# A causal mask taken from TensorE to POOL's select, with new turns for all engines

## The chip, the cores and the metric

The kernel runs on one core of a Trainium2 chip. The metric is device time in microseconds (us) from one launch; lower is better. All times are of that core.

## The reference

A residual stream `x` of 2048 tokens and 128 features goes through four layers. Each computes `x = x + s * silu(f)`, where `s` and `f` are two branches on the layer-normalised `x`.

- Layer 0: `s` is a Mamba-2 block; `f` a mixture of 8 experts (2 per token) with 2 shared experts, all with biases.
- Layer 1: `s` is gated linear attention; `f` a feed-forward with ternary weights.
- Layer 2: gated linear attention; and again 8 experts, 2 per token, with a shared one.
- Layer 3: `s` is causal softmax attention with rotary positions, 16 heads of 8 features, over sequences of 256 tokens; `f` is a short gated recurrence and an output projection.

What the change touches is the attention of layer 3:

```
scores = einsum('bhqd,bhkd->bhqk', q, k) * hd ** -0.5
mask   = where(kpos > qpos, -inf, 0)
attn   = softmax(scores + mask, axis=-1)
out    = einsum('bhqk,bhkd->bhqd', attn, v) ; out = out @ Wo.T
```

and, in layer 0, the sum of the experts' second biases, weighted by the gates, and the shared experts' biases.

## The kernel before

**Tiling and order.** Tokens go in four blocks (`tb`) of 512 per layer, each of two sequences of 256 (`bb`). Every engine has its program as a set of named streams of Python generators; a `yield` ends a turn. The strings in `ORDER` say, engine by engine, which stream takes the next turn and how many ("Y3" is three turns of stream Y), and `follow` deals them out. So each engine's instruction order is fixed beforehand, across layers, and engines meet only by semaphores. `T`, `S`, `V`, `G` are the counters of TensorE, ScalarE, VectorE and POOL (GpSimd). A turn beyond a stream's end, and the first turn of each part of a chain, issue nothing. The streams that matter: A (input side of the attention branch), B (its output side), F (the `f` branch and experts), R and C (sending rows to the experts, fetching them back), M (`peaks3`), Y (`attn3`); on sync, H moves layer 3's heads through DRAM and M its maxima.

**Layer 3's attention.** `heads3` computes rotated queries and keys, splits them into bf16 parts and sends them through DRAM (`part`, SP lines L2391 and L2413) into the head layout `qp`, `kp`. The head buffers of block `tb` are those of `tb - 2`, so the trip of a later block waits for the last score unit of that block. `peaks3` (TensorE L744 to L769, VectorE L1966) computes the masked scores once to find each row's maximum: score products L754 and L760, mask products L756 and L761 (identity times `mts[0]`, which adds -1e30), one VectorE reduction L1971 for each unit. The maxima travel by DMA into rows 72 and 73 of `qp`, so that the second pass has them subtracted in its product.

`attn3` is the second pass. A block has 24 units: for each of two sequences `bb` and four groups `g` of four heads, `k` = 0 and 1 (two heads each, 256 queries by the first 128 keys) and `k` = 2 (four heads, second half by second half). A unit is one turn of scores into bank 3 or 6, transposed (keys on rows): L782 or L788, with the mask product L784 or L789 (`mts[1]`) on each diagonal block. ScalarE takes the exponential into one of four tiles `PT` (L1278). `values` has a turn for each unit: nothing for `k` = 0, for `k` = 1 the products L800 (four heads in four 32-column strips of the array, side by side, into bank 7), for `k` = 2 the products L805. The ninth value column is one, which yields the softmax's sum. ScalarE copies bank 7 out (L1285), TensorE turns it (L814, `norm`), VectorE divides (L1997, L2002). At a block's end `tail` transposes (L521) and multiplies by Wo (L529). `used_up` says when an exponential may overwrite its `PT` tile.

**Layer 3's recurrence** is L989, L990 on TensorE with ScalarE L1407 to L1412 and VectorE L2122 to L2127; its last part is L1418 and L1420.

**Between layers 2 and 3.** POOL fetches expert answers row by row with indirect DMAs (`fetch`, L2270, 16 for each half of the tokens); VectorE mixes them by the gates (L2081), ScalarE takes the tanh of the gate (L1298), VectorE updates `x`. From 640 us on POOL has three rsqrt steps (L2171, L2175) and nothing else.

**Layer 0's bias.** In `shared`, before the second products L854 of each of four chunks, L851 multiplies `cmT` (10 rows: eight gate weights and two ones, by token) with `bias0` (10 x 128). 16 such products in the kernel, two records each.

## Time and profile before

| what | value |
|---|---|
| time, median of 3 runs | 764.8 us (761.33, 764.8, 766.14) |
| profiled execution, first to last instruction | 796.7 us |
| TensorE busy | 691.7 us (87%) |
| VectorE busy | 500.9 us (63%) |
| ScalarE busy | 439.9 us (55%) |
| POOL busy | 252.8 us (32%) |
| mean granted TensorE clock | 0.931 of 2.4 GHz |

The profiled execution is longer than the timed ones; its span is the time against which its durations add up. PE is TensorE, ACT ScalarE, DVE VectorE, SP the sync engine. Busy time counts pipelined matmuls up to their modelled ends, so the time from one start to the next says more about their cost than their duration. A releaser after `<-` is the instruction whose end ended the idle time.

### The profile page before, as it was taken

To read this page: it belongs to the slowest core of one execution; us is meant where nothing else is said; L and a number is where in the kernel's file an instruction comes from. 1 tells how busy PE (TensorE), PEld (TensorE's weight loads), DVE (VectorE), ACT (ScalarE), POOL (GpSimd) and SP (SyncE) were. 2 spreads that over 40 slices of the span, in tenths; PEclk is the share of its full clock that TensorE was granted. 3 is DMA by queue.
4 is the path that set the end of the run, shared out by engine and by line. 5 is a ranking of instruction groups with operands and counts; after the bars stand their busy time and mean duration, and the time that the engine had idled before them with its cause. 6 is when DMAs were issued, how large, how long until landed. Compare 5 with 4: busy or idle time off the path is not lost.

```text
span 796.7 us, 13833 instructions
## 1 busy us (share of the span) xinstructions
PE 691.7 (87%) x5174; PEld 538.4 (68%) x5174; DVE 500.9 (63%) x1333; ACT 439.9 (55%) x944; POOL 252.8 (32%) x267
## 2 busy tenths in 40 slices
PE   7699898899888689899799993989877699999996
PEld 4377666578766567677679983789756466767663
DVE  1747877449965774868643863447646568767652
ACT  4535787449884665685535652134541265655554
POOL 1473456552515812323650326354000520000000
PEclk9679999999999897999989997889998889999998
DMA  9721654126301130000126662427894603306100
GB/s 305 226 63 32 180 145 140 42 87 176 91 24 44 50 124 1 1 0 2 34 89 220 209 196 70 163 77 225 262 250 135 154 15 101 62 21 143 28 17 14
DMA packets 71217, 83.94 MB, mean 105 GB/s; under 512 B 7199, under 2 KB 55914, under 8 KB 71146
## 3 DMA queue, kind: packets, MB, share of 16 engines
q1 hardware_dynamic: 67054, 74.65, 32.3%
q0 software_dynamic: 4096, 8.40, 3.5%
q8 instruction: 41, 0.67, 0.3%
q14 instruction: 26, 0.21, 0.1%
HBM read 65.46 MB, written 17.43 MB: 104 GB/s over the span
## 4 chain that ended last, share of the span: by engine, by line
PE 64%; DVE 10%; ACT 9%; DMA 6%; issue 4%; POOL 4%; another core or an unknown queue 1%; SPq 0%; ACTq 0%; POOLq 0%; DVEq 0%
PE bank L854 4%; PE bank L842 4%; PE bank L922 4%; PE bank L713 4%; PE bank L931 4%; PE bank L690 2%; PE bank L667 2%; PE bank L529 2%; DMA part<-arena 2%; PE bank L896 2%; PE bank L800 2%; PE bank L782 2%; PE bank L659 2%; PE bank L958 2%; DMA W<-part 2%
## 5 line engine op out<-in xcount | busy, mean ns | idle before, releaser
L1971 DVE TENSOR_REDUCE arena<-bank 128x2 f32<-128x512 f32 (+1 forms) x96 | 63.7, 684 | 25.7 <-PE bank L756 15.7
L1278 ACT ACTIVATE arena<-bank 128x512 f32<-128x512 f32 x96 | 55.8, 597 | 34.0 <-PE bank L784 27.3
L931 PE MATMUL bank<-room,h 128*128 128x128 f32 x368 | 50.6, 281 | 4.8 <-DVE h L2054 1.6
L922 PE MATMUL bank<-room 128*128 128x128 f32 x368 | 50.3, 282 | 2.6 <-DMA room<-in_wx 2.5
L931 PEld LDWEIGHTS bank<-room,h 128*128 128x128 f32 x368 | 46.0, 195 | 7.7 <-issue 3.3
L922 PEld LDWEIGHTS bank<-room 128*128 128x128 f32 x368 | 46.3, 197 | 5.3 <-DMA room<-in_wx 3.6
L1374 ACT ACTIVATE h<-bank,room 128x128 f32<-128x128 f32 x96 | 27.3, 368 | 27.3 <-PE bank L922 18.1
L2270 POOL DMA_INDIRECT win<-answer,arena x24 | 23.6, 984 | 57.9 <-DMA answer<-room 38.4
L2255 POOL DMA_INDIRECT sent<-own,arena x32 | 32.5, 1015 | 27.7 <-DVE arena L1647 18.8
L2171 POOL TENSOR_SCALAR rs<-mv 128x4 f32<-128x4 f32 x20 | 7.3, 363 | 105.5 <-DVE mv L1459 82.0
L2255 POOL DMA_INDIRECT sent<-own,room x32 | 36.1, 1128 | 12.0 <-issue 8.3
L1915 DVE TENSOR_TENSOR arena<-bank,cst 128x512 f32<-128x512 f32 x32 | 21.1, 686 | 28.9 <-remote 11.1
L1305 ACT ACTIVATE h<-bank,col 128x512 f32<-128x512 f32 x24 | 16.3, 686 | 40.3 <-PE bank L842 24.7
L1737 DVE SCALAR_TENSOR_TENSOR arena<-arena,col 128x512 f32<-128x512 f32 x48 | 35.4, 770 | 3.4 <-ACT arena L1094 3.4
L2270 POOL DMA_INDIRECT room<-answer,room x32 | 32.6, 1017 | 14.4 <-issue 8.1
L2054 DVE TENSOR_SCALAR h<-bank,room 128x128 f32<-128x128 f32 x88 | 24.7, 343 | 16.2 <-PE bank L922 13.2
L713 PE MATMUL bank<-xt,arena 128*128 128x64 f32 (+1 forms) x128 | 19.0, 299 | 16.3 <-DVE arena L1915 13.5
L713 PEld LDWEIGHTS bank<-xt,arena 128*128 128x128 f32 x128 | 19.2, 226 | 20.6 <-DVE arena L1915 15.5
L1337 ACT ACTIVATE h<-bank,room 128x128 f32<-128x128 f32 x92 | 26.6, 382 | 3.6 <-PE bank L886 3.4
L1247 ACT ACTIVATE arena<-bank 128x512 f32<-128x512 f32 (+1 forms) x16 | 7.8, 489 | 36.9 <-PE bank L713 36.9
L2175 POOL TENSOR_TENSOR sc<-sc,mhalf 128x16 f32<-128x16 f32 (+1 forms) x12 | 27.8, 2317 | 0.9
L896 PE MATMUL bank<-room,h 128*128 128x128 f32 x184 | 27.0, 293 | 1.0 <-ACT room L1346 1.0
(413 smaller groups left out, 2059.1 us busy)
## 6 DMA issues: line engine op xcount, KB each, us to landing
room<-in_wx SPq DMA_DIRECT2D x46, 578.0 KB
room<-in_wx SPq DMA_DIRECT2D x46, 257.0 KB, 2.8
answer<-room SPq DMA_DIRECT2D x44, 128.0 KB
room<-sent SPq DMA_DIRECT2D x20, 256.0 KB
W<-part SPq DMA_DIRECT2D x12, 384.0 KB
room<-part SPq DMA_DIRECT2D x12, 384.0 KB
sent<-acc SPq DMA_DIRECT2D x10, 256.0 KB, 4.3
part<-arena SPq DMA_DIRECT2D x12, 128.0 KB
```

What stands on the lines that cost most here:

```text
L713: mm = pe.matmul(b[:, o + dv * h:o + dv * h + dv], AT[:, h, c, :], vv[:, c, dv * h:dv * h + dv], start=(q == 0), stop=(q == 0 or h == 3))
L842: mm = pe.matmul(b[:], w1[:, q // nh, width(q % nh)], src[:], start=True, stop=True)
L854: mm = pe.matmul(o, hid(l, tb, q)[:, width(c)], w2[:, q // nh, q % nh, :], start=(q == 0 and l == 2), stop=(q == 3))
L896: mm = pe.matmul(b[:, width(i)], hid(0, "x", u)[:, width(2 * i + j)], zw2[slots(0, v)][:, j, :], start=(j == 0), stop=(j == 1))
L922: mm = pe.matmul(b[:, width(j)], xw1[slots(2, u)][:, width(j)], xsT[(s // 2) % 2][:, width(s % 2)], start=True, stop=True)
L931: mm = pe.matmul(banks[6][:, width(s % 2)], hid(2, "x", u)[:, width(j)], xw2[slots(2, u)][:, j, :], start=(j == 0), stop=(j == 3))
L1278: act.activation(PT[n % 4], banks[(3, 6)[n % 2]][:], ACT.Exp).then_inc(*S.step("PT", tb, n))
L1737: dve.scalar_tensor_tensor(out=xj, in0=raw[:, j, :, k:k + 256], scalar=K("conv_w", 4 * j + k), in1=xj, op0=ALU.mult, op1=ALU.add).then_inc ...
L1971: dve.tensor_reduce(mx[:, tb % 2, bb, int(k < 2), h:h + nh], banks[1 + n % 2][:].rearrange("p (h t) -> p h t", h=nh), AX.X, ALU.max).then_ ...
L2175: pool.tensor_tensor(dst, dst, mhalf[:, 0:src.shape[1]], ALU.pow).then_inc(*G.step(*name))
L2255: pool.indirect_dma_start(sent[h], bass.IndirectOffsetOnAxis(ap=place[l, h][:, n:n + 1], axis=0), own[:, h, n % 8, :], None).then_inc(*DMA ...
L2270: pool.indirect_dma_start(gx[l][4 * k + c], None, answer[h], bass.IndirectOffsetOnAxis(ap=place[l, h][:, n:n + 1], axis=0)).then_inc(*DMA[ ...
```

## The change

1. **The mask of `attn3`.** L784 and L789 are gone; the score products now end their accumulation. POOL has a new stream Y: behind each exponential it runs `affine_select` in place on the diagonal blocks of the `PT` tile (2 blocks of 128 columns for `k` = 0 and 1, 4 for `k` = 2), which writes zero where the key is later than the query. `peaks3` keeps its mask products; one mask tile `mts` is left.
2. **Value products.** `values(i)` is one turn per group: all eight products, behind the select of the group's third unit. It stands behind the scores of unit 3i + 5 (before: behind those of 3i + 3 and 3i + 4). `norm(i)` stands behind the scores of unit 3i + 8. `PT` has six tiles (`N_P`), `used_up` counts groups, and ScalarE's copy of bank 7 stands behind the exponential of unit 3i + 6.
3. **Biases over 128 rows.** `cmT` and `bias0` have 128 rows, of which 118 are zero; POOL clears `cmT` once at the start, between two other fills; the product runs over 128 rows.
4. **New turns.** All five strings of `ORDER` are new from their first entry to their last. Tensor has 957 turns instead of 1021 (Y 169 instead of 233), pool 396 instead of 295 (Y, new, has 101), scalar 757, vector 1057 and sync 227 as before, with the same number for each stream. The diff shows only the ends of two of the strings.

```diff
     "tensor": steps(
...
-        "M2 Y4 M2 Y4 M1 Y1 M1 Y2 M1 Y2 M1 Y3 M1 Y2 M2 Y4 F1 M2 Y3 M1 Y2 M1 Y1 M1 Y1 M1 Y1 M2 Y1 M1 Y1 M1 Y2 M1 Y24 M1 "
-        "Y31"),
+        "M2 Y4 M2 Y3 M1 Y3 M3 Y3 M1 Y2 M1 Y1 M1 Y1 M2 Y1 M1 Y1 M1 Y1 M1 Y2 M2 Y4 M1 Y3 M1 Y19 F1 Y12 "),
...
     "pool": steps(
...
-        "A1 C6 A1 C5 R1 C3 B1 C1 B1 A4 C1 A3 C5 A2 C12 A7"),
+        "A6 B2 F3 R8 A1 R4 A1 R1 A1 R4 A1 B2 A1 C1 A5 B2 A2 R12 B2 R1 C1 R1 A1 R2 C5 A1 C7 B2 C3 A7 C3 F1 C7 A1 C1 Y3  "
+        "C1 Y1 C2 A1 Y3 C1 Y2 A1 Y1 A1 N1 C1 Y1 C1 Y6 A1 Y7 A2 Y1 A1 Y7 C1 Y9 D1 Y7 R1 Y39 A1 Y13 "),
...
+N_P = 6
...
-        bias0 = sb("bias0", [10, 128])
+        bias0 = sb("bias0", [128, 128])
...
         PT = [carve(512) for i in range(4)]
...
+        PT += [carve(512) for i in range(N_P - 4)]
         idb = sb("idb", [128, 128], BF16)
-        mts = [sb(f"mts{i}", [128, 128], BF16) for i in range(2)]
+        mts = sb("mts", [128, 128], BF16)
...
-        cmT = sb("cmT", [10, TB])
+        cmT = sb("cmT", [128, TB])
...
         def used_up(tb, n):
-            tb, u = (tb, n - 4) if n >= 4 else (tb - 1, n + 20)
-            return T.end("av", tb, u + (UNITS[u][2] == 0))
+            tb, u = (tb, n - N_P) if n >= N_P else (tb - 1, n + 24 - N_P)
+            return T.end("av", tb, u // 3)
...
                             pe.matmul(b[:, 256 * e:256 * e + 256], qp[0:72, h, o + 128:o + 256], kp[0:72, h, o:o + 256],
                                       start=True, stop=False)
-                            mm = pe.matmul(b[:, 256 * e + 128:256 * e + 256], idb[:], mts[0][:], start=False, stop=True)
+                            mm = pe.matmul(b[:, 256 * e + 128:256 * e + 256], idb[:], mts[:], start=False, stop=True)
...
@@ -779,32 +786,28 @@
                     if k < 2:
                         for e in range(2):
                             h = 4 * g + 2 * k + e
-                            pe.matmul(b[:, 256 * e:256 * e + 256], kp[0:74, h, o:o + 128], qp[0:74, h, o:o + 256],
-                                      start=True, stop=False)
-                            mm = pe.matmul(b[:, 256 * e:256 * e + 128], idb[:], mts[1][:], start=False, stop=True)
+                            mm = pe.matmul(b[:, 256 * e:256 * e + 256], kp[0:74, h, o:o + 128], qp[0:74, h, o:o + 256],
+                                           start=True, stop=True)
                     else:
                         for e in range(4):
                             h = 4 * g + e
-                            pe.matmul(b[:, width(e)], kp[0:74, h, o + 128:o + 256], qp[0:74, h, o + 128:o + 256], start=True, stop=False)
-                            mm = pe.matmul(b[:, width(e)], idb[:], mts[1][:], start=False, stop=True)
+                            mm = pe.matmul(b[:, width(e)], kp[0:74, h, o + 128:o + 256], qp[0:74, h, o + 128:o + 256],
+                                           start=True, stop=True)
                     mm.then_inc(*T.step("st", tb, n))
 
-                def values(n):
-                    bb, g, k = UNITS[n]
+                def values(i):
+                    bb, g = i // 4, i % 4
                     by = banks[7][:, 0:256]
-                    T.wait_ge(*S.end("PT", tb, n))
-                    if k == 1:
-                        take(7, S, "w", tb, n // 3)
-                        for e in range(4):
-                            p = PT[(n - 1 + e // 2) % 4]
-                            mm = pe.matmul(by[32 * e:32 * e + 9, :], v9[:, 2 * bb, 4 * g + e, :], p[:, 256 * (e % 2):256 * (e % 2) + 256],
-                                           start=True, stop=False, tile_position=(0, 32 * e))
-                        mm.then_inc(*T.step("av", tb, n))
-                    if k == 2:
-                        for e in range(4):
-                            mm = pe.matmul(by[32 * e:32 * e + 9, 128:256], v9[:, 2 * bb + 1, 4 * g + e, :], PT[n % 4][:, width(e)],
-                                           start=False, stop=True, tile_position=(0, 32 * e))
-                        mm.then_inc(*T.step("av", tb, n))
+                    take(7, S, "w", tb, i)
+                    T.wait_ge(*G.end("causal", tb, 3 * i + 2))
+                    for e in range(4):
+                        p = PT[(3 * i + e // 2) % N_P]
+                        pe.matmul(by[32 * e:32 * e + 9, :], v9[:, 2 * bb, 4 * g + e, :], p[:, 256 * (e % 2):256 * (e % 2) + 256],
+                                  start=True, stop=False, tile_position=(0, 32 * e))
+                    for e in range(4):
+                        mm = pe.matmul(by[32 * e:32 * e + 9, 128:256], v9[:, 2 * bb + 1, 4 * g + e, :], PT[(3 * i + 2) % N_P][:, width(e)],
+                                       start=False, stop=True, tile_position=(0, 32 * e))
+                    mm.then_inc(*T.step("av", tb, i))
 
                 def norm(i):
                     b = take(5, V, "norm", tb, i)
@@ -824,11 +827,11 @@
                     if n < 24:
                         scores(n)
                         yield
-                    if 2 <= n < 26:
-                        values(n - 2)
-                        yield
-                    if n >= 6 and n % 3 == 0:
+                    if n >= 8 and n % 3 == 2:
                         norm(n // 3 - 2)
+                        yield
+                    if 5 <= n < 29 and n % 3 == 2:
+                        values(n // 3 - 1)
                         yield
                 yield from tail(3, tb, 1, wa3[:, 5:6, :], (3, 6), "norm", tb, 7)
...
                 for c in range(4):
                     o = b[:, width(c)]
                     if l == 0:
-                        pe.matmul(o, cmT[0:10, width(c)], bias0[:], start=True, stop=False)
+                        pe.matmul(o, cmT[:, width(c)], bias0[:], start=True, stop=False)
...
                 if tb >= 2:
-                    S.wait_ge(*T.end("av", tb - 2, 23))
+                    S.wait_ge(*T.end("av", tb - 2, 7))
...
             def attn3(l, tb):
-                for n in range(24 + 4):
+                for n in range(24 + 6):
                     if n < 24:
                         S.wait_ge(*T.end("st", tb, n))
-                        if n >= 4 or tb:
+                        if n >= N_P or tb:
                             S.wait_ge(*used_up(tb, n))
-                        act.activation(PT[n % 4], banks[(3, 6)[n % 2]][:], ACT.Exp).then_inc(*S.step("PT", tb, n))
-                        yield
-                    if n >= 4 and n % 3 == 1:
-                        i = (n - 4) // 3
-                        S.wait_ge(*T.end("av", tb, 3 * i + 2))
+                        elif n >= 4:
+                            S.wait_ge(*T.end("o", 2, 3, 1))
+                        act.activation(PT[n % N_P], banks[(3, 6)[n % 2]][:], ACT.Exp).then_inc(*S.step("PT", tb, n))
+                        yield
+                    if n >= 6 and n % 3 == 0:
+                        i = n // 3 - 2
+                        S.wait_ge(*T.end("av", tb, i))
                         S.wait_ge(*(T.end("norm", tb, i - 2) if i >= 2 else T.end("norm", tb - 1, i + 6) if tb else T.end("yzT", 2, 3, 0)))
                         w = yz[:, 2 * (i % 2):2 * (i % 2) + 2, 128:256]
                         act.copy(w, banks[7][:, 0:256].rearrange("p (q t) -> p q t", q=2)).then_inc(*S.step("w", tb, i))
...
                 for tb in (2 * h, 2 * h + 1):
                     yield
+                    V.wait_ge(*G.end("cmT"))
                     V.wait_ge(*T.end("cm", tb))
                     V.wait_ge(*T.since(tb, "second", 0, tb - 1))
-                    dve.tensor_copy(cmT[:], banks[2][0:10, :]).then_inc(*V.step("cmT", tb))
+                    dve.tensor_copy(cmT[0:10, :], banks[2][0:10, :]).then_inc(*V.step("cmT", tb))
...
             def masks():
                 V.wait_ge(*DMA["cst"].all())
                 dve.tensor_copy(idb[:], ident)
-                dve.tensor_tensor(mts[0][:], upper, ident, ALU.subtract).then_inc(*V.step())
-                t = V.here()
-                yield
-                V.wait_ge(*t)
-                dve.tensor_scalar(mts[0][:], mts[0][:], -1e30, None, ALU.mult)
-                dve.tensor_scalar(mts[1][:], lower, -1e30, None, ALU.mult).then_inc(*V.step("mask"))
+                dve.tensor_tensor(mts[:], upper, ident, ALU.subtract).then_inc(*V.step())
+                t = V.here()
+                yield
+                V.wait_ge(*t)
+                dve.tensor_scalar(mts[:], mts[:], -1e30, None, ALU.mult).then_inc(*V.step("mask"))
...
+
+            def attn3(l, tb):
+                for n, (bb, g, k) in enumerate(UNITS):
+                    e = 2 if k < 2 else 4
+                    p = PT[n % N_P].rearrange("p (e t) -> p e t", e=e)[:, :, 0:128]
+                    G.wait_ge(*S.end("PT", tb, n))
+                    pool.affine_select(p, p, [[0, e], [1, 128]], ALU.is_ge, 0.0, base=0, channel_multiplier=-1).then_inc(*G.step("causal", tb, n))
+                    yield
...
             pool.memset(acc[:], 0.0).then_inc(*G.step("zero"))
             pool.memset(mhalf[:], -0.5)
             pool.memset(raw[:, :, :, 0:3], 0.0).then_inc(*G.step("pad"))
+            pool.memset(cmT[:], 0.0).then_inc(*G.step("cmT"))
             pool.memset(cm2[:], 1.0).then_inc(*G.step("cm2"))
             pool.memset(ones[:], 1.0).then_inc(*G.step("ones"))
...
+                "Y": chain(attn3(3, tb) for tb in range(4)),
...
-        "bias0": np.concatenate([a["L0_ffn_b2"], a["L0_ffn_sb2"]], axis=0),
+        "bias0": np.concatenate([a["L0_ffn_b2"], a["L0_ffn_sb2"], np.zeros((118, 128), np.float32)], axis=0),
...
```

## Rows read from the trace of the kernel before

**Rows 1.** busy time by stage; columns: stretch, length, each engine, clock, DMA

```profile
0.00:577.00 577.00, 500.51 (x3194) 400.26 (x3195) 365.32 (x1013) 332.45 (x720) 234.29 (x247) 0.93 0.37 113
...
640.00:765.00 125.00, 122.28 (x1333) 87.09 (x1334) 90.17 (x212) 70.72 (x144) 3.57 (x6) 0.99 0.25 58
...
765.00:787.00 22.00, 20.96 (x282) 12.33 (x280) 7.54 (x22) 17.22 (x35) 0.00 (x0) 1.00 0.06 15
```

**Rows 2.** timeline of TensorE: start us, us, engine, line, operation

```profile
769.28 0.27 PE L782 MATMUL bank<-room 74*128 74x256 bf16 x1
...
769.56 0.22 PE L784 MATMUL bank<-mts,idb 128*128 128x128 bf16 x1
...
769.71 0.62 PE L800 MATMUL bank<-arena 128*9 128x256 f32 x8
...
770.26 0.44 PE L814 MATMUL bank<-cst,yz 128*128 128x128 f32 x2
...
770.97 0.41 PE L805 MATMUL bank<-arena 128*9 128x128 f32 x8
...
771.30 0.23 PE L788 MATMUL bank<-room 74*128 74x128 bf16 x1
...
771.78 0.27 PE L782 MATMUL bank<-room 74*128 74x256 bf16 x1
```

**Rows 3.** chain of waits, 612 to 640: start us, us, what

```profile
624.80 8.89 DMA wout<-answer,arena
...
635.84 0.63 ACT th L1298
...
636.46 0.49 ACT arena L1278
```

**Rows 4.** groups of instructions on TensorE, 577 to 797

```profile
L784 PE MATMUL bank<-mts,idb 128*128 128x128 bf16 x128 | 26.1, 227 | 0.0
...
L789 PE MATMUL bank<-mts,idb 128*128 128x128 bf16 x128 | 18.6, 223 | 0.0
```

**Rows 5.** chain of waits, 134 to 142

```profile
135.88 1.09 PE bank L854 x8
...
136.97 0.41 PE bank L851 x2
```

**Rows 6.** groups of instructions on POOL, whole span

```profile
L2192 POOL TENSOR_TENSOR W<-cst,dtb 128x512 f32<-128x512 f32 x16 | 18.7, 1173 | 18.7 <-PE bank L565 11.8 <-DVE dtb L1727 6.9
...
L2235 POOL MEMSET arena<- 128x576 f32 x1 | 0.6, 577 | 4.1 <-ACT nT L1080 4.1
```

**Rows 7.** one line of POOL: duration ns, min/median/max

```profile
L2201 POOL TENSOR_TENSOR arena<-xt,col x16: 721/840/1176, 57.0 to 211.5; 128x256 f32<-128x256 f32 x16
```

**Rows 8.** timeline of ScalarE, last stretch

```profile
771.57 0.37 ACT L1285 COPY yz<-bank 128x256 f32<-128x256 f32 x1
...
771.98 1.08 ACT L1278 ACTIVATE arena<-bank 128x512 f32<-128x512 f32 x2
...
773.58 0.60 ACT L1278 ACTIVATE arena<-bank 128x512 f32<-128x512 f32 x1 [0.51 <-PE bank L784]
```

**Rows 9.** timelines of ScalarE and TensorE, end of the attention

```profile
786.49 0.37 ACT L1285 COPY yz<-bank 128x256 f32<-128x256 f32 x1 [0.89 <-PE bank L805]
...
787.01 0.41 PE L814 MATMUL bank<-cst,yz 128*128 128x128 f32 x2 [0.58 <-ACT yz L1285]
```

**Rows 10.** groups of instructions on VectorE, 577 to 797

```profile
L1971 DVE TENSOR_REDUCE arena<-bank 128x2 f32<-128x512 f32 x64 | 42.9, 682 | 14.8 <-PE bank L756 13.5 <-PE bank L761 0.7
```

**Rows 11.** chain of waits, whole span

```profile
729.50 8.74 DMA room<-part
```

**Rows 12.** who waited for whom, whole span: us in total, times, longest

```profile
DVE arena L1915 <- remote: 11.1, 1, 11.1
```

**Rows 13.** timeline of POOL, 612 to 640

```profile
629.14 0.94 POOL L2270 DMA_INDIRECT win<-answer,arena  x1 [3.40 <-DVE own L2081]
...
639.11 0.95 POOL L2270 DMA_INDIRECT wout<-answer,arena  x1 [0.30 <-issue]
```

6 lines of the change are left out of this document (3 added, 3 removed), and 111 rows, old and new, of the table ORDER.

## The prediction

> **What bounds the kernel now.** I read the busy time by stage first [rows 1]. The last layer's attention and its gated recurrence fill 640 to 787 us. In 640:765 TensorE is busy 122.28 of 125 us, VectorE 90.17, ScalarE 70.72, POOL 3.57; in 765:787, where only the attention of the last token block is left, TensorE 20.96 of 22, ScalarE 17.22, POOL nothing. Busy can hide pipelining, so I went to the timeline of TensorE [rows 2]: one group of four heads takes 769.28 to 771.78 = 2.50 us, and its instructions follow each other without a hole. TensorE is the bound there, and POOL is free. Ahead of 640 it is different: the chain of waits [rows 3] runs over the fetches of the expert answers (landing 8.89 us), ScalarE's L1298 and then the first exponentials at 636.46, which stand behind L1298 in ScalarE's order. This change takes nothing off that piece.
>
> The profiled execution spans 796.7 us, 31.9 us (4.2%) over the median of 764.8. I make the sum against 796.7 and carry it over by the ratio 764.8/796.7 = 0.960.
>
> **Mask products removed.** L784 and L789 are 128 + 128 mask products in the score turns of `attn3` [rows 4]. The eight instructions of a third unit, four of them masks, take 771.30 to 771.78 = 0.48 us, so 0.06 each [rows 2]. A group has 2 + 2 + 4 = 8 masks, 0.48 us; 32 groups (4 blocks of 8) make **15.4 us**. The 256 masks of `peaks3` stay. TensorE issues in order and is the bound from 637 on, so these lie on the path. Bounds: all 15.4, or half, should another engine take over at once (VectorE's 90 of 125 and ScalarE's 71 of 125 say it does not).
>
> **One turn of value products per group.** The products into 32-row strips stand between full-width products. L800 (256 columns) starts 0.09 after the last mask's slot (769.56 + 0.06 to 769.71) and holds the engine 0.55, 0.64 in all; L805 (128 columns) with the same 0.09 lead holds it 0.33 (770.97 to 771.30), 0.42 in all [rows 2]. The difference, 0.22, is what 128 columns cost, so a turn has 0.20 us that is no column. One turn instead of two saves 0.20 x 32 = **6.4 us**. Bounds 0 (the break between the two halves stays) and 6.4; I take 6.4, since nothing full-width stands between the halves any more. The Trainium skill (TensorEngine Tiling (Array Packing), on mode switching) says that a change of tiling mode drains the engine; by that rule the saving is real, and the 0.20 of the row agrees.
>
> **Bias of layer 0 over 128 rows.** L851 with 10 rows takes 0.41 in the chain, the eight records of L854 behind it 1.09 for four products, 0.27 each [rows 5]. If a full-height product costs 0.27 there, 0.14 x 16 = 2.2 us. Bounds 0 and 2.2; TensorE is busy 500.51 of 577 us in these layers [rows 1], so I take **1.5**. The zero fill of `cmT` on POOL (a fill of 576 columns is 0.58 [rows 6]) delays the fills behind it, `ones` among them, by 0.5 at the start; the normalisation of the first block needs POOL only later, so nothing. The load of `bias0` grows from 5 to 64 KB and is asked for long after: nothing. One mask tile less to prepare: nothing, VectorE has slack.
>
> **POOL's select, added.** There are 96, two of 256 and one of 512 elements per row in each group; no row shows one. Nearest: a fill (write only) of 576 at 0.58, and the two-input products, 0.72 to 1.18 with a median of 0.84 for 256 [rows 7] and 1.17 mean for 512 [rows 6]. Bounds for a group: 2 x 0.26 + 0.52 = 1.0 (1.0 ns per element by the fill), and 2 x 0.84 + 1.17 = 2.9. A select reads one stream, so I take the middle, 2.0 (0.6, 0.6, 0.8). Over 637:787 that is 32 x 2.0 = 64 of 150 us on an engine that does nothing else after 640. It is hidden behind TensorE because the values of group i are asked for when the scores of unit 3i + 5 are out, and six `PT` tiles instead of four let the exponentials run on. What is behind it in POOL's queue: the last six fetches of layer 2 and three normalisations. What isn't hidden is the end: the last exponential now goes through a select of 512 (0.8) and a values turn of 0.86 instead of 0.42: **+1.2 us**. The Trainium skill (GPSIMD Engine Reference, Engine selection) speaks against the move: elementwise work belongs to VectorE, though it has one-input work at about line rate; at its 1.2 GHz a group would be an estimated 0.9 us, and the sum would gain 0.3 at the end.
>
> **What is late next.** In the last stretch a group would be 2.50 - 0.48 - 0.20 = 1.82 us on TensorE, while ScalarE needs 0.41 (copy) + 1.08 (two exponentials) + 0.49 (the third) = 1.98 [rows 8]. The change also adds waits: the values turn stands for bank 7 (copy of the group before, which ScalarE issues behind its next exponential) and for the third select, and behind it on TensorE wait the next scores; that exponential waits in turn for the values. The loop is 0.86 (values) + 0.54 (exponential) + 0.41 (copy) + 0.15 (a hop from copy to TensorE, 786.49 + 0.37 to 787.01 [rows 9]) = 1.96, no more than ScalarE's own 1.98. The new order leaves 31 Y turns behind the last M turn, 18 score units, 6 groups: 6 x 0.16 = **+1.0 us**. In 640:765 I take 15% off the 21.8, **+3.3 us**, for two places: VectorE's 96 reductions of 0.68 [rows 10] then fill more of each peaks stage, and the trip of the last block's heads through DRAM, whose second half alone is 8.74 us [rows 11], leaves TensorE with less other work per microsecond. The order holds 17 M and 21 Y turns over that trip, where before it held 10 and 18, so it is largely covered.
>
> **New turns in layers 0 to 2.** All five orders are new from the first entry. Lengths are equal except Y on tensor (233 to 169) and on pool (0 to 101). I can't price these; the end of layer 2 is nearly in the same order (the turns of H on sync, and of Y and M, stand beside nearly the same counts of the others). I take 0, and for the range the largest stall of that part, 11.1 us [rows 12], as what an order may hit or miss, halved: 5.5 either way.
>
> **Sum.** 15.4 + 6.4 + 1.5 - 1.2 - 1.0 - 3.3 = 17.8 us. 796.7 - 17.8 = 778.9 in the profile; x 0.960 = **748 us**.
>
> **Rivals.**
> 1. POOL becomes the bound of the last stretch. At 2.9 us a group, 6 groups cost 6 x (2.9 - 1.98) = 5.5 more and the end 0.4: gain 11.9, 784.8, 753 us. For: the two-input rows of 256 reach 1.18 [rows 7], which shows POOL being slowed at times. Against: a select has one input. The Trainium skill (GPSIMD Engine Reference, Key points) names contention with VectorE instructions that read two SBUF inputs; by that it would come from the recurrence's and the rope's products, which the last stretch hardly has. Chance 0.14.
> 2. The time of TensorE is given back by other waits: half of 21.8 is realised (VectorE in the peaks stages, the trip through DRAM). 15.4 + 6.4 halved, + 1.5 - 1.2 - 1.0: gain 10.2, 786.5, 755 us. For: VectorE is at 72% in 640:765 and would be at 82% of the shortened stretch. Against: TensorE hardly waits there today. Chance 0.17.
> 3. Slower: POOL's queue as a wait for TensorE. The selects stand in POOL's order between the last fetches (C63 behind the selects of units 0 to 2, C65 behind that of unit 3), and the fetches wait for VectorE's mixing: 3.40 us before 629.14, and the last of them goes out at 639.11, 10 us later [rows 13]. TensorE waits in order for the select of unit 2, then 5. If it stands through both these 10 us and a landing of 8.89 [rows 3], 18.9 us, with the work that overlapped them gone, it outweighs the 17.8: 797.8; with a restart at the half clock of 1.2 GHz, which costs as much again for a few us of work (say 5), 802.8, 771 us. It decides from 17.8 us of such standing. Against: the exponentials themselves wait for L1298 until 636.46, so much of it is time that is lost today. Chance 0.08.
> 4. The new turns of layers 0 to 2 move the time by themselves, 1.5% (11 us) either way: 737 or 759 us. Chance 0.07 each.
> 5. That the masks are not in fact gone can't be: the diff drops them.
>
> The forecast keeps 0.47. **Range** 737 to 764: it takes in rivals 1, 2 and most of 4, and leaves rival 3 and the far ends out. 1% (7.6 us) is about what a measurement of this kernel tells from no change; below 757.2 counts as faster, above 772.4 as slower. Faster: 0.47 + 0.14 + 0.12 (most of rival 2) + 0.07 = 0.80, less 0.03 for unknown errors of the method: 0.77. Slower: rival 3 when it is large and a bad order, 0.08. The rest, 0.15, is within 1%.
>
> **What would show it.** Right: a group of the last stretch at about 2.0 us instead of 2.50, with ScalarE without holes; one values turn at about 0.86; L851's successor at 0.27 in the chain; selects at about 0.6 and 0.8, POOL busy some 65 us after 637; the stretch from the first exponentials to the last at 133 instead of 150 us; the first 577 us within 6. Wrong: values turns that wait for POOL, a group at 2.9, VectorE as the releaser in the chain from 640 on, or the start of the last layer moved by more than 6 us.

## The result, and the profile after

The kernel before takes 764.45 us, the changed kernel **733.91 us** (medians of five runs each; 761.33 to 766.14 and 732.28 to 738.58). The ratio is 0.9609, 95% interval 0.9578 to 0.9641: **faster by 30.5 us**. Forecast were 748 us and a range from 737 to 764, so the direction was right and the size wrong: 30.5 us came where I had counted 17. Some executions of a kernel take over 1.5% more than its fastest one, at a lower granted clock; the ratios leave them out, and `values_late`, with four such runs of six, has none.

The first profile of before (796.7 us) lies far above its timed runs, so it was taken again (below, `before_again`). That one spans 764.5 us, the changed kernel's 737.3. To set two executions beside each other, a mark in the work helps. Mine is the first of the last sixteen fetches of layer 2 on POOL, those of its second half (the expectations below call them the last eight): what follows is, but for a rest of layer 2, the last layer. Busy time by stage, columns as in [rows 1], first the changed kernel, then before.

```profile
0.00:568.90 568.90, 503.19 (x3393) 406.28 (x3394) 374.35 (x1054) 338.54 (x746) 228.79 (x248) 0.96 0.43 128
568.90:737.30 168.40, 148.43 (x1527) 104.93 (x1525) 117.42 (x279) 94.04 (x196) 67.40 (x116) 0.93 0.29 68
```

```profile
581.60:764.50 182.90, 163.35 (x1768) 114.11 (x1768) 115.04 (x275) 96.01 (x194) 18.32 (x20) 0.95 0.27 63
```

Read the lengths first: the mark comes at 568.9 instead of 581.6, 12.7 us sooner, and behind it stand 168.4 us instead of 182.9, 14.5 fewer. Together 27.2, the whole difference of the two spans. Then read the first busy column: TensorE has 14.9 us less to do behind the mark (163.35 to 148.43), and stands idle for 20.0 and 19.5 us. The time of the last layer went where its work went. POOL's busy time rises from 18 to 67 us.

The group of four heads in the last stretch, TensorE's timeline, which answers [rows 2] and [rows 4]:

```profile
711.18 0.62 PE L805 MATMUL bank<-arena 128*9 128x256 f32 x8
...
711.95 0.61 PE L789 MATMUL bank<-room 74*128 74x256 bf16 x4
713.03 0.40 PE L794 MATMUL bank<-room 74*128 74x128 bf16 x4 [0.47 <-ACT arena L1283]
713.38 0.41 PE L817 MATMUL bank<-cst,yz 128*128 128x128 f32 x2
713.72 0.62 PE L805 MATMUL bank<-arena 128*9 128x256 f32 x8
```

From one start of L805 to the next: 2.54 us. I had forecast 2.0, from 2.50 before. The values turn holds the engine 0.77 us (711.18 to 711.95) where I had 0.86. TensorE is no longer full here; it waits 0.47 us for an exponential. The chain of waits over the same group says what closes the loop:

```profile
711.25 0.55 PE bank L805 x8
711.80 0.22 PE bank L808 x8
712.02 0.34 PE bank L789 x2
...
712.38 0.61 ACT arena L1283
...
713.03 0.40 PE bank L794 x4
713.43 0.37 PE bank L817 x2
713.79 0.55 PE bank L805 x8
```

Values, first scores, exponential, third scores, norm, values. POOL's select is not in it. What the select costs, and who waits for it (min/median/max ns; it answers [rows 6, 7]):

```profile
L2250 POOL TENSOR_SCALAR_AFFINE_SELECT arena<-arena x96: 406/408/1093, 582.6 to 724.6; 128x256 f32<-128x256 f32 x64, 128x512 f32<-128x512 f32 x32
its engine sat idle before it (us, times) until:
  ACT arena L1283: 74.4, 62
who waited for it (us, times):
  PEld bank L805: 1.3, 4
```

408 ns is the usual select of 256; one of 512 takes 0.64 us (row under select_twice). POOL waits 74.4 us for ScalarE, and is waited for 1.3 us in all (by PEld, the weight loads of the value products).

The exponentials of the last layer, changed and before (duration min/median/max in ns, then the first and the last start):

```profile
L1283 ACT ACTIVATE arena<-bank x96: 576/597/624, 581.9 to 723.9; 128x512 f32<-128x512 f32 x96
```

```profile
L1278 ACT ACTIVATE arena<-bank x96: 578/597/626, 594.8 to 752.8; 128x512 f32<-128x512 f32 x96
```

From the first to the last start it is 142.0 us instead of 158.0. I had forecast 133 instead of 150. Both numbers were too small, since I took 636.46 for the first exponential, which in that profile starts at 630.7. The difference, 16.0, is near the 17 that they implied.

The bias of layer 0, which answers [rows 5], in TensorE's timeline of the changed kernel:

```profile
127.52 0.39 PE L854 MATMUL bank<-bias,cmT 128*128 128x128 f32 x2
...
128.63 0.39 PE L854 MATMUL bank<-bias,cmT 128*128 128x128 f32 x2
```

A column block takes 1.11 us (127.52 to 128.63), where [rows 5] had 0.41 + 1.09 = 1.50: 0.39 less, not 0.14.

### The profile page after: what moved, and what is told of

It reads as the page before. It is cut to its first block, busy times and chain, and to the rows that moved or that the text cites. A ratio compares the mean times of both kernels' runs of the same rounds, so it can differ in the third digit from the quotient of the medians.

```text
span 737.3 us, 13432 instructions
## 1 busy us (share of the span) xinstructions
PE 651.6 (88%) x4918; PEld 511.2 (69%) x4918; DVE 491.8 (67%) x1332; ACT 432.6 (59%) x942; POOL 296.2 (40%) x364
## 4 chain that ended last, share of the span: by engine, by line
PE 57%; ACT 13%; DVE 10%; DMA 8%; POOL 6%; issue 4%; SPq 1%; ACTq 0%; POOLq 0%; DVEq 0%
PE bank L925 4%; PE bank L934 4%; PE bank L720 3%; DMA room<-in_wx 3%; PE bank L536 2%; PE bank L857 2%; PE bank L674 2%; PE bank L697 2%; POOL sent L2268 2%; PE bank L845 2%; PE bank L572 2%; DMA W<-part 2%; PE bank L899 2%; PE bank L666 2%; PE bank L805 2%
## 5 line engine op out<-in xcount | busy, mean ns | idle before, releaser
L2250 POOL TENSOR_SCALAR_AFFINE_SELECT arena<-arena 128x256 f32<-128x256 f32 (+1 forms) x96 | 49.0, 513 | 76.4 <-ACT arena L1283 74.4
L1977 DVE TENSOR_REDUCE arena<-bank 128x2 f32<-128x512 f32 (+1 forms) x96 | 63.6, 682 | 23.2 <-PE bank L768 12.3
L934 PE MATMUL bank<-room,h 128*128 128x128 f32 x368 | 49.7, 278 | 5.5 <-DVE h L2060 4.2
L934 PEld LDWEIGHTS bank<-room,h 128*128 128x128 f32 x368 | 45.1, 192 | 7.8 <-DVE h L2060 4.6
L2283 POOL DMA_INDIRECT room<-answer,room x32 | 34.6, 1082 | 22.5 <-DMA answer<-room 14.5
L2176 POOL TENSOR_SCALAR rs<-mv 128x4 f32<-128x4 f32 x20 | 5.1, 253 | 93.9 <-DVE mv L1464 65.9
L2268 POOL DMA_INDIRECT sent<-own,arena x32 | 32.7, 1021 | 24.7 <-DVE arena L1653 15.9
L1743 DVE SCALAR_TENSOR_TENSOR arena<-arena,col 128x512 f32<-128x512 f32 x48 | 39.5, 840 | 1.3 <-ACT arena L1097 1.2
L899 PEld LDWEIGHTS bank<-room,h 128*128 128x128 f32 x184 | 24.2, 201 | 6.8 <-ACT room L1351 4.6
L899 PE MATMUL bank<-room,h 128*128 128x128 f32 x184 | 26.3, 287 | 2.8 <-ACT room L1351 2.8
L1332 ACT ACTIVATE room<-bank,col 128x256 f32<-128x256 f32 (+1 forms) x24 | 11.1, 464 | 30.0 <-PE bank L876 30.0
L1041 ACT ACTIVATE arena<-x,nm,rs 128x128 f32<-128x128 f32 x48 | 19.7, 484 | 11.9 <-DVE nm L1468 10.2
```

Source lines behind the costliest of these rows:

```text
L899: mm = pe.matmul(b[:, width(i)], hid(0, "x", u)[:, width(2 * i + j)], zw2[slots(0, v)][:, j, :], start=(j == 0), stop=(j == 1))
L934: mm = pe.matmul(banks[6][:, width(s % 2)], hid(2, "x", u)[:, width(j)], xw2[slots(2, u)][:, j, :], start=(j == 0), stop=(j == 3))
L1743: dve.scalar_tensor_tensor(out=xj, in0=raw[:, j, :, k:k + 256], scalar=K("conv_w", 4 * j + k), in1=xj, op0=ALU.mult, op1=ALU.add).then_inc ...
L1977: dve.tensor_reduce(mx[:, tb % 2, bb, int(k < 2), h:h + nh], banks[1 + n % 2][:].rearrange("p (h t) -> p h t", h=nh), AX.X, ALU.max).then_ ...
L2250: pool.affine_select(p, p, [[0, e], [1, 128]], ALU.is_ge, 0.0, base=0, channel_multiplier=-1).then_inc(*G.step("causal", tb, n))
L2268: pool.indirect_dma_start(sent[h], bass.IndirectOffsetOnAxis(ap=place[l, h][:, n:n + 1], axis=0), own[:, h, n % 8, :], None).then_inc(*DMA ...
```

## The experiments

Ratios are to runs of the kernel before on the same chip. The runs came in four sets, each on a chip of its own. Before took 765.5 us in the first (before_again, early_new, mask_tensor, bias_10), 763.5 in the second (early_old, late_old, values_two, pt_8), 811.8 in the third and 764.3 in the last. The third chip was slower, so runs of that set are compared with the changed kernel in it. Those of the first two are compared with the first result, 0.9609. The changed kernel has 0.9509 and 0.9551 on the other two chips, so a difference of two ratios from different sets may be off by some 4 us more than its interval says. "The stretch" is the part from the mark to the end. The stretch and the marks are from one profile each.

| kernel | median us | ratio, 95% interval | mark at | stretch | TensorE busy in it |
|---|---|---|---|---|---|
| before_again | 765.75 (one run) | | 581.6 | 182.9 | 163.4 |
| changed | 733.91 | 0.9609, 0.9578 to 0.9641 | 568.9 | 168.4 | 148.4 |
| early_new | 758.82 | 0.9913, 0.9880 to 0.9946 | 572.8 | 181.2 | 163.0 |
| early_old | 745.27 | 0.9750, 0.9717 to 0.9782 | 577.9 | 166.3 | 147.1 |
| mask_tensor | 744.73 | 0.9727, 0.9696 to 0.9758 | 563.0 | 175.6 | 156.2 |
| values_two | 740.08 | 0.9689, 0.9650 to 0.9727 | 563.8 | 171.1 | 151.0 |
| bias_10 | 736.59 | 0.9614, 0.9576 to 0.9653 | 571.2 | 166.8 | 145.3 |
| late_old | 753.11 | 0.9863, 0.9835 to 0.9890 | 571.6 | 183.1 | 151.1 |
| pt_8 | 732.93 | 0.9602, 0.9558 to 0.9645 | 561.0 | 167.2 | 146.0 |
| third set: after_again | 769.30 | 0.9509, 0.9455 to 0.9563 | 597.6 | 166.9 | 146.1 |
| late_old_mask | 797.06 | 0.9843, 0.9777 to 0.9910 | 608.6 | 188.1 | 163.3 |
| order_only | 788.01 | 0.9750, 0.9692 to 0.9808 | 600.1 | 186.5 | 165.4 |
| select_twice | 786.02 | 0.9713, 0.9661 to 0.9765 | 605.5 | 179.3 | 155.0 |
| last set: after_third | 733.86 | 0.9551, 0.9500 to 0.9603 | 573.0 | 167.4 | 145.4 |
| pt_8_again | 734.89 | 0.9611, 0.9575 to 0.9648 | 561.1 | 166.0 | 144.4 |
| values_late | 742.07 | none | 564.6 | 166.5 | 145.9 |

Six kernels with the changed last layer (changed, early_old, bias_10, pt_8, after_again, after_third) have stretches of 166.3 to 168.4 us, mean 167.2, on the slower chip too (pt_8_again, not in the mean, has 166.0). Before has 182.9, and 182.0 in the first profile (614.7 to 796.7). So the stretch is a sharper measure than the whole run, whose layers 0 to 2 scatter by several us: the same early turns put the mark at 561.0 to 573.0.

A part of the stretch is sharper still. Every kernel has 96 exponentials of the last layer, 24 for each token block, in the same order. From the start of the 25th to the start of the 96th the granted clock is 1.00 in every run but select_twice (0.95). Ahead of it are fetches and stretches at half clock, behind it the end of the kernel. From ScalarE's timelines, in us:

| kernel | mark to 25th | 25th to 96th | 96th to end |
|---|---|---|---|
| before_again | 67.0 | 104.2 | 11.7 |
| early_new | 66.4 | 104.1 | 10.7 |
| the six, and pt_8_again | 59.3 to 61.3 | 93.8 to 94.1 | 12.1 to 13.3 |
| mask_tensor | 61.6 | 101.9 | 12.1 |
| values_two | 60.2 | 98.6 | 12.3 |
| order_only | 67.3 | 106.7 | 12.4 |
| late_old | 69.8 | 98.7 | 14.5 |
| late_old_mask | 69.5 | 105.7 | 13.0 |
| select_twice | 64.6 | 100.3 | 14.4 |

The middle column repeats within 0.4 us from chip to chip, so I read the prices of single edits from it (24 of the 32 groups of heads lie in it), with 93.9 for the changed last layer and 104.0 for the old one.

**before_again.** No edit.

> The kernel before, unchanged, for a second profile, since the one shown spans 796.7 us and its timed runs take 764.5. If the 30 us are stalls of that one execution, this one spans about 763, its layers 0 to 2 end some 25 to 30 us sooner, and from the first exponentials of the last layer to its last stays at 150 us (637 to 787 in the profile shown). Then of the 30.5 us of the change, what the last layer gives is 150 us less its length after, about 143 measured the same way, so 7 to 12, and the rest was won in layers 0 to 2. Rival: the last layer is also 5 or more us shorter here, 145 or less; then my sum for the last layer was made against a stretch that was disturbed itself.

It spans 764.5. The first profile of before had its mark at 614.7 and 182.0 us behind it, this one 581.6 and 182.9. So the last layer against which I summed was sound, and the 32 us too many lay ahead of it. The rival, a last layer that was disturbed itself, falls: its middle part takes 103.8 us in the first profile and 104.2 in this one. The gain of the last layer is larger than the 7 to 12 that I gave there, for I had measured the two from different points.

**early_new**: the old kernel with the new turns of layers 0 to 2.

```diff
 # code as before
-ORDER[engine] = old turns
+ORDER[engine] = new turns to a place behind the last send of layer 2, then the old ones
```

> The kernel before with the changed kernel's turns in layers 0 to 2 and its own turns in the last layer (masks on TensorE, two value turns, bias of 10 rows, no select). Theory 1, the step that failed is 'new turns in layers 0 to 2: I take 0': most of what I missed is here, 13 to 19 us off 764.5, so 746 to 752, ratio 0.975 to 0.983. Theory 2, the turns of layers 0 to 2 move nothing and the last layer gives more than I summed: within 4 us of 764.5, 760 to 768.

6.7 us faster (0.9913): real, and half of the least that theory 1 asked (13 to 19). The stretch behind the mark is that of before (181.2), the mark comes 8.8 us sooner. The place where the old turns take over lies ahead of the mark, so the last part of layer 2 is in the old order here.

**early_old**: the reverse.

```diff
-ORDER[engine] = new turns
+ORDER[engine] = old turns up to the same place, then the new ones
```

> The changed kernel with the old turns in layers 0 to 2 (every engine follows the order of before until the first turns of the last layer's attention) and its new turns from there on. The new turns put into the old kernel gave 6.7 us (0.9913). Theory 1, the parts add: 0.9609 + 0.0087, ratio 0.970, 742 us, with the last fetches of layer 2 ending some 8 us later. Theory 2, the new early turns are worth more where the last layer is ready to use the time, since in the changed kernel the first exponential starts 12.9 us sooner than in before and in early_new only 7.5: 0.977 or more, 747 us and up. Rival: less than 3 us, the early turns are worth nothing here.

0.9750 against 0.9609: the early turns are worth 1.4% here, 10.8 us, give or take 3.5 and what the chips differ by. That lies between the two theories, and the stretch (166.3) is that of the changed kernel: all that is lost is lost ahead of the mark. Both runs together show that the turns of layers 0 to 2 move the time. I had put them at 0.

Where? Marks on POOL's timeline: the last fetch of layer 0, the first and the last send of layer 2, the first of the last sixteen fetches.

| kernel | fetch L0 | first send | last send | mark | L0 fetch to mark |
|---|---|---|---|---|---|
| before_again | 262.7 | 370.1 | 477.8 | 581.6 | 318.9 |
| early_old | 256.7 | 365.9 | 473.6 | 577.9 | 321.2 |
| early_new | 261.6 | 358.1 | 475.1 | 572.8 | 311.2 |
| late_old | 256.6 | 355.6 | 473.7 | 571.6 | 315.0 |
| changed | 259.7 | 360.8 | 477.2 | 568.9 | 309.2 |
| mask_tensor | 255.3 | 354.6 | 471.5 | 563.0 | 307.7 |
| values_two | 255.8 | 354.6 | 472.0 | 563.8 | 308.0 |
| pt_8_again | 255.3 | 353.2 | 469.2 | 561.1 | 305.8 |

Layer 0 gives nothing that stands out of the scatter. Layer 1 brings the first send 6 to 13 us sooner than in the two old orders, counted from the fetch of layer 0, and the sends give most of it back (107.7 us from the first to the last before, 116 to 118 after): the new order moves work behind them. What stays is won between the last send and the mark: 104 us in before and in early_old, 97.7 and 97.9 where the old turns take over on the way, 91.4 to 92 where the new ones go through. Early_old has the new turns on the second part of that way, and they give nothing there without those ahead of them. So 320 us become 313 by the early turns and 308 by all the new turns: **12 us ahead of the mark**, the number missing from my sum. These are single profiles. The other four runs with all the new turns on a fast chip (bias_10, pt_8, after_third, values_late) have 304.5 to 314.2 us from fetch to mark, so the 12 may be off by several us. Which move in the order does it, no run tells.

**mask_tensor**: the 256 lower masks back on TensorE.

```diff
-mm = pe.matmul(b[:, 256*e:256*e+256], kp[...], qp[...], start=True, stop=True)
+pe.matmul(b[:, 256*e:256*e+256], kp[...], qp[...], start=True, stop=False)
+mm = pe.matmul(b[:, 256*e:256*e+128], idb[:], mt2[:], start=False, stop=True)
 ...
-T.wait_ge(*G.end("causal", tb, 3 * i + 2))
+T.wait_ge(*S.end("PT", tb, 3 * i + 2))
```

> The changed kernel with the 256 lower masks of the exponentials back on TensorE and no selects on POOL; its turns, one value turn per group, six PT tiles and the bias of 128 rows stay. By my sum the masks are worth 15.4 less 0.8 (select at the end) and less two thirds of the 3.3 and 1.0 that I took off, so about 11.5: 745.5 us. Theory 2 (the last layer gives all of the unexpected gain): 18 or more, 752 and up. Rival 2 of the prediction (other waits give TensorE's time back): 5 to 7, 739 to 741. With the loop that the trace after shows in the last stretch (values, exponential, third scores, norm, values, 2.54 us a group), a group there should be 2.54 + 0.24 for the four masks of the third unit, about 2.8.

0.9727 against 0.9609, 9.0 us of 764.5, give or take 3.4; the stretch 175.6 against 167.2, 8.4 us. Expected were 11.5 net out of 15.4 gross, and the interval of the time reaches to that. Busy times don't decide it: 156.2 against a mean of 146.4 over the six kernels is 9.8, but work at half clock is busy for longer, and from the mark to the 25th exponential this run has a clock of 0.97 where the six have 0.89 to 0.94. The middle part does, at 1.00 in both: 101.9 against 93.9, 8.0 us for 24 groups, 0.33 each, where I had 0.48. A group of the last stretch takes 2.77 us here (714.72 to 717.49), as the expectation had it (2.8). A third unit with its masks, in TensorE's timeline of this kernel:

```profile
713.52 0.28 PE L790 MATMUL bank<-room 74*128 74x256 bf16 x1
...
713.87 0.27 PE L790 MATMUL bank<-room 74*128 74x256 bf16 x1
...
714.72 0.23 PE L796 MATMUL bank<-room 74*128 74x128 bf16 x1 [0.35 <-ACT arena L1285]
...
715.20 0.39 PE L819 MATMUL bank<-cst,yz 128*128 128x128 f32 x2
```

And one without, from the middle of the changed kernel's last layer:

```profile
692.40 0.39 PE L794 MATMUL bank<-W 74*128 74x128 bf16 x4
692.62 0.39 PE L817 MATMUL bank<-cst,yz 128*128 128x128 f32 x2
```

With four masks 714.72 to 715.20 = 0.48 us. Without, 713.03 to 713.38 = 0.35 in the last stretch (above), but 692.40 to 692.62 = 0.22 here. In five of the six groups where the third scores had waited 0.3 us or more for an exponential, the norm products start 0.35 behind them. Of the other 26, 14 have 0.22 or 0.23 to whatever stands behind them. So four masks cost 0.13 in the last stretch, 0.03 each, and 0.06 each, as in my sum, where it is 0.22. In the first two units (0.35 for two scores and two masks, 713.52 to 713.87 here, against 2 x 0.112, from the 0.61 of four records less the 0.27 of one, divided by three) a mask costs 0.063. Over all 32 groups, from each start to the next and without the waits, third units take 15.4 us here and 9.3 in the changed kernel, first and second units 23.5 and 16.4: 13.3 us gross instead of 15.4. The difference to the net 8 to 9 goes into waits. I had taken one group, where nothing waited, for all.

**values_two**: the value products of a group in two pieces around the norm.

```diff
+first_half(n // 3 - 1)    # 256-column products
 norm(n // 3 - 2)
 yield
-values(n // 3 - 1)
+second_half(n // 3 - 1)   # 128-column products
 yield
```

> The changed kernel with the value products of a group in two pieces again: the 256-column products stand ahead of the full-height norm products and the 128-column ones behind them, in the same turns. It puts back one break between full-width work and 32-row strips in 31 of 32 groups. My term, 0.20 x 32 = 6.4, less 15%: 5.4 slower, 739.5 us, ratio 0.968. Rival: the break is hidden or costs only its 0.09 of lead, 0 to 2.5 us. Rival: 12 us or more, which would make this the term that I mis-sized.

0.9689: 6.1 us slower, give or take 4; stretch 4 us longer; the middle part 4.7 us longer, 0.20 for each of its 24 groups. Near the 5.4 expected, and the term of 6.4 stands. The Trainium skill (TensorEngine Tiling (Array Packing), Tiling Modes, Key Properties) says that changing the mode drains the engine. This run agrees in so far as the extra change costs time: 4 to 6 us for 31 breaks, 0.13 to 0.20 us each.

**bias_10**: ten rows again.

```diff
-pe.matmul(o, cmT[:, width(c)], bias0[:], start=True, stop=False)
+pe.matmul(o, cmT[0:10, width(c)], bias0[:], start=True, stop=False)
```

> The changed kernel with the bias product of layer 0 over 10 rows again; all else as changed. My term: 1.5 us slower, bounds 0 and 2.2, so 735.4 us against 733.9. Theory 1b: the term is larger, because a product of 10 rows holds up the full-height one behind it and the chain of layer 0 goes through it in all four blocks: 3 us or more. Rival: 0, within 0.7 us, since the waits of layers 0 to 2 take it up.

0.9614 against 0.9609: 0.4 us, give or take 3.8. No effect that this measurement can tell. TensorE's timeline of this kernel shows that the work itself was there:

```profile
130.05 0.48 PE L854 MATMUL bank<-bias,cmT 10*128 10x128 f32 x2
...
131.55 0.48 PE L854 MATMUL bank<-bias,cmT 10*128 10x128 f32 x2
```

1.50 us a column block against 1.11 with 128 rows, 0.39 x 16 = 6.2 us of TensorE's time, above my bound of 2.2. How much of it comes out in the time stays open: the interval and what the chips differ by could hide it.

**late_old**: the old interleaving of the last layer under the changed code.

```diff
-ORDER["tensor"] = new turns
+ORDER["tensor"] = new turns to a place behind the last send of layer 2, then the old ones,
+                  of the Y turns only scores, second values and norm
 # scalar, vector, sync likewise; POOL's order stays the changed one
```

> The changed kernel, its new turns in layers 0 to 2 kept, with the old turns in the last layer: tensor's Y turns stand where the same score, second value and norm turns stood, the two other value turns are dropped; POOL's order is the changed one. What this costs is the worth of the new order of the last layer. Of the 30 us, 6.7 are the early turns, about 9 the masks, 0 to 1 the bias, at most 6.4 the joined value turns; so theory 1 says that about 8 are this order: 742 us, ratio 0.971. Rival: 0 to 3 us, 734 to 737, and the joined value turn or the six PT tiles are worth more than I summed.

0.9863: 19.4 us slower than the changed kernel, where 8 were expected and 0 to 3 by the rival. No other single edit to the changed kernel costs as much. TensorE has only 151.1 us to do, little more than in the changed kernel, and is idle for 32.0 of the 183.1 us instead of 20. So under the old order the code edits free TensorE and the stretch doesn't get shorter: 181.2 in early_new, 183.1 here. The table of parts says where it goes: the middle part falls from 104.1 to 98.7 us, about half of the 10 that it falls under the new order, and the parts around it give it back, 3.4 us ahead of it and 3.8 behind. Its chain around 590:

```profile
581.57 9.37 DMA wout<-answer,arena
...
590.96 1.15 DVE own L2108 x4
...
592.13 0.63 ACT th L1324
592.76 0.49 ACT arena L1304
...
593.31 0.67 POOL arena L2271
...
594.13 1.21 POOL win L2304
```

A fetch, mixing, exponential, a select, and behind the select the next fetch: the place that my third rival named. And the waits of TensorE in the stretch, longest first:

```profile
PE bank L796 <- DVE arena L1998: 8.3, 4, 6.3
PE bank L815 <- ACT arena L1304: 6.6, 15, 0.8
```

L796 turns the maxima. It waits once for 6.3 us, until 592.75, since VectorE's reduction L1998 stands behind the mixing L2108, and that behind the landing of the fetches. From 588 to 605 the granted clock is then 0.50. That wait is no work of the selects: early_new, without any, has one of 5.6 us at the same place, with a shorter time at half clock behind it. L815 is the third score unit; it waits 15 times for an exponential, 6 times and 2.7 us in the changed kernel. What the selects add was left to late_old_mask.

**late_old_mask**: late_old with the masks on TensorE and no selects.

```diff
 # ORDER of late_old, POOL without its Y turns; masks as in mask_tensor
```

> late_old (changed code, old turns in the last layer) with the masks back on TensorE and no selects. late_old took 753 us, ratio 0.9863; from the first of the last eight fetches of layer 2 to the end it takes 183.1 us, as before does (182.9), and TensorE is idle for 32.0 of them where before, early_old, mask_tensor and the changed kernel have 19 to 20. Its chain runs from an exponential over a select (593.31) to a fetch (594.13), and the granted clock around it is 0.70. Theory 1: the selects between the fetches in POOL's order (my third rival) eat what the masks gave: without selects TensorE gets 8 us more to do and gives back 10 or more of idle time: 178 to 183 us for that stretch, ratio 0.979 to 0.986, no slower than late_old. Theory 2: the old interleaving itself is bad for joined value turns and six tiles, selects or not: masks add their 8 us, 190 us for the stretch, ratio 0.997 and above.

Stretch 188.1, TensorE busy 163.3, idle 24.8. That is between the theories (178 to 183, and 190), nearer the second. Its ratio, 0.9843, lies in the range of the first, but that range was made with 0.9609 for the changed kernel, which has 0.9509 on this chip. Over the changed kernel of its set it is 1.036 (797.06 over 769.30), late_old over the changed kernel 1.026. The same code under the new order, mask_tensor, has a stretch of 175.6. So 12.5 of the 15.9 us between late_old and the mean 167.2 come from the old interleaving with joined value turns and six tiles, selects or not. The selects' share is the rest, 3.4 by a difference of single profiles: about 1 us in each of the three parts. Ahead of the 25th exponential, where the fetches are, it is 69.8 with selects and 69.5 with masks in their place. The third rival's mechanism can be seen in the chain and is small; that it costs time is argued from this difference, not shown.

**order_only**: the new turns, masks on TensorE, value products in two pieces.

```diff
 # the edits of mask_tensor and of values_two together
```

> The changed kernel with masks on TensorE, no selects, and the value products in two pieces around the norm products: of the change only the new turns (all layers), the six tiles and the 128-row bias are left. If the parts add: mask_tensor 0.9727 plus the 0.0080 of values_two, ratio 0.981, 749 us, and the last stretch (from the first of the last eight fetches) 175.6 + 4.0 = 179.6 us. Rival: the pieces are hidden once TensorE has the masks again, or the other way round: off by 4 us or more from 749.

0.9750, and 788.01 over 769.30 is 1.024, 18.7 us, where mask_tensor and values_two alone cost 9.0 and 6.1. The intervals allow the sum. The stretch is 186.5 instead of 179.6, but the middle part adds to a tenth: 106.7 less 93.9 is 12.8, and the two alone have 8.0 and 4.7. What is over lies ahead of the 25th exponential (67.3 against 60.2 to 61.6), in a single profile and on the slower chip, and its cause is open. So the prices of masks and value turns stand, and a third number falls out: with masks and two value pieces the new order takes 106.7 us for the middle part where the old one takes 104.0. There the new turns (with six tiles) cost 2.7 us, and the new code pays 12.7 to gain 10.1. The new order without the new code is no faster in the last layer than before was (182.9), so the order alone doesn't give the 15 us.

**after_again.** No edit; the reference of the third set.

> The changed kernel itself, beside the others of this call, as the reference for them and for a second profile. Ratio 0.961 again, within 0.004. If the stretch from the first of the last eight fetches to the end is what the other runs of the same last layer show (166.2 to 168.4 us), it spans 166 to 169 here too, and differences between runs of this kernel lie in layers 0 to 2.

0.9509, below the 0.957 that was the edge of the expectation. The stretch is 166.9, as expected. So on the slower chip the changed kernel's last layer takes as long as ever, and its layers 0 to 2 take longer. The gain there is 42.5 us instead of 30.5; that the rest of it lies in layers 0 to 2 is likely and not shown, for before has no profile on that chip.

**select_twice**: every select done twice.

```diff
+pool.affine_select(p, p, ...).then_inc(*G.step())
+G.wait_ge(*G.here())
 pool.affine_select(p, p, ...).then_inc(*G.step("causal", tb, n))
```

> The changed kernel with every select done twice, one after the other, so POOL has 49 us more to do and each PT tile is ready 0.43 or 0.67 us later, plus the semaphore between. Theory 1, POOL is hidden: only the end pays, one select of 512, 0.7 to 1 us, and a little where the values of a group wait: under 3 us, ratio 0.961 to 0.965. Rival 1 of the prediction, POOL at 2.9 us a group bounds the last stretch: two rounds of 1.53 plus gaps are 3.2 us a group against 2.54, six or seven groups, 4 to 5 us there, and more where fetches of layer 2 queue behind selects: 6 us or more.

16.7 us slower than after_again, stretch 179.3 against 166.9. Theory 1 is refuted as far as "hidden" meant with room to spare. TensorE's timeline of the last stretch:

```profile
753.48 0.62 PE L805 MATMUL bank<-arena 128*9 128x256 f32 x8 [0.40 <-POOL arena L2252]
...
756.43 0.62 PE L805 MATMUL bank<-arena 128*9 128x256 f32 x8 [0.34 <-POOL arena L2252]
...
760.17 0.62 PE L805 MATMUL bank<-arena 128*9 128x256 f32 x8 [1.12 <-POOL arena L2252]
...
763.37 1.04 PE L805 MATMUL bank<-arena 128*9 128x256 f32 x8
...
767.03 1.04 PE L805 MATMUL bank<-arena 128*9 128x256 f32 x8
```

In POOL's timeline the selects follow each other all but without a gap, one of 512 among them:

```profile
759.49 0.64 POOL L2252 TENSOR_SCALAR_AFFINE_SELECT arena<-arena 128x512 f32<-128x512 f32 x1
760.07 0.41 POOL L2250 TENSOR_SCALAR_AFFINE_SELECT arena<-arena 128x256 f32<-128x256 f32 x1
```

A group takes 2.95 us (753.48 to 756.43): almost exactly the 2.9 of my first rival, for two selects a tile. And then something follows that no sum of mine had. Busy time of the same part, in four pieces:

```profile
740.00:750.00 10.00, 8.56 (x99) 6.53 (x96) 7.02 (x14) 4.20 (x8) 3.48 (x8) 1.00 0.11 29
750.00:758.00 8.00, 5.72 (x73) 2.89 (x73) 2.99 (x9) 4.75 (x11) 7.52 (x16) 1.00 0.02 5
758.00:764.00 6.00, 4.33 (x40) 2.12 (x44) 0.95 (x5) 3.38 (x8) 5.59 (x13) 0.73 0.00 0
764.00:776.00 12.00, 9.96 (x84) 4.14 (x76) 2.72 (x10) 5.39 (x12) 7.87 (x16) 0.57 0.07 22
```

The column behind POOL's is the granted clock: 1.00 while TensorE was busy for 8.56 of 10 us and for 5.72 of the next 8, 0.73 in the piece behind them and 0.57 from 764 on. It fell within the third piece, in which TensorE waited 1.12 us for a select (until 760.17). At 1.2 GHz the same eight value products take 1.04 us instead of 0.62 and a group 3.66 (763.37 to 767.03), and in these groups TensorE no longer waits for POOL. The wait for POOL thus costs a second time, by the clock. Of the 12.4 us, 3.6 lie ahead of the 25th exponential, where selects stand between the fetches, 6.5 in the middle part and 2.3 behind it.

**pt_8** and **pt_8_again**: eight PT tiles.

```diff
-N_P = 6
+N_P = 8
 ...
+PT += [xt[:, 2 * i:2 * i + 2, :].rearrange("p a t -> p (a t)") for i in range(2)]
```

> The changed kernel with eight PT tiles instead of six (two more in a buffer of layer 1 that is free by then). In the trace after, a group of the last stretch takes 2.54 us and not 2.0, and I read that as a loop: value products, the exponential of unit 3i + 6 (which waits for its tile), the third score unit (its bank), norm, values. With eight tiles that exponential needs only the values of the group before. If the loop is the bound, a group falls to ScalarE's own 3 x 0.60 + 0.37 = 2.2, 6 or 7 groups, 2 us, and a little in the middle: 731 to 732, ratio 0.956 to 0.958. Rival: the loop closes elsewhere (the two banks of scores) and nothing moves, within 1 us of 733.9.

> The changed kernel with eight PT tiles, again beside its successor and its reference. If the loop closes over the banks it equals the changed kernel, ratio 1.000 within 0.004, and a group of the last stretch is 2.54 us; if the tiles gave something in the middle of the last layer, 0.998 or less.

0.9602 against 0.9609, and on the last chip 734.89 us against the changed kernel's 733.86: nothing (the ratios there are 0.9611 and 0.9551, with intervals that overlap). The middle part is 93.8 in both. In the chain of pt_8 a group still takes 2.55 us: 703.47 0.55, 704.02 0.22, 704.24 0.34, 704.60 0.61, 705.25 0.40, 705.65 0.36, then 706.02. The tiles were not what closed the loop; my first reading of the trace was wrong. By the chain it is the two score banks: the third scores need the bank of an exponential that could only start behind the values.

**values_late**: pt_8, and in the last token block norm and values behind the second score unit instead of ahead of the first.

```diff
+late = 2 if tb == 3 else 0
+m = n - late
-if n >= 8 and n % 3 == 2: norm(n // 3 - 2)
+if m >= 8 and m % 3 == 2: norm(m // 3 - 2)
 ...
 # values(m // 3 - 1) likewise; ScalarE's copy one exponential later
```

> The changed kernel with eight PT tiles, and in the last token block the norm and value turns of a group stand one score unit later pair: behind the second score unit of the group after the next instead of ahead of its first, ScalarE's copy one exponential later. In the changed kernel and in pt_8 a group of the last stretch takes 2.54 us, and the chain there reads 0.55 + 0.22 (values), 0.34 (first two scores), 0.61 (exponential), 0.40 (third scores), 0.37 (norm). Theory: the loop closes over the two score banks (the third scores wait for the exponential that could start only behind the values), which is why eight tiles alone did nothing. With the values between the second and the third scores, TensorE works while that exponential runs: a group falls to ScalarE's 3 x 0.60 + 0.38, 2.2 us; 6 to 8 groups, 2 to 2.7 us less than pt_8 and the changed kernel, ratio to the changed kernel 0.996 to 0.997. Rival: the copy, now behind another exponential, makes the next value turn wait, and the group stays at 2.5: no gain.

The third scores no longer wait. The second ones (L790) now wait 0.47 us for the bank of an exponential, and that stands behind the copy, the rival's place:

```profile
714.54 0.55 PE bank L806 x8
715.09 0.26 PE bank L809 x8
...
715.38 0.37 ACT yz L1294
715.75 0.53 ACT arena L1287
...
716.33 0.39 PE bank L790 x2
716.72 0.22 PE bank L818 x2
716.94 0.55 PE bank L806 x8
```

714.54 to 716.94 is 2.40 us, 0.14 less than 2.54 and not the 2.2 expected. The loop was not opened: it still closes over a score bank, and the copy came into it. The last block as a whole gained nothing: from its first exponential to its last it takes 18.3 us, in pt_8 and the changed kernel 18.1. The six runs took 731 to 745 us, which settles nothing. No version beat the changed kernel.

**after_third.** No edit; the reference of the last set.

> The changed kernel as the reference for values_late and pt_8_again on the same chip, ratio to before between 0.950 and 0.962 as on the two chips so far. The time before on this chip says which of two things is true of layers 0 to 2: where before takes 764, the ratio should be 0.961; where it takes 810, 0.951.

0.9551, with before at 764.29 and single runs from 724.6 to 741.7. The rule "764 gives 0.961" is not confirmed; its interval reaches from 0.950 to 0.9603. The gain of the changed kernel is 4 to 5%. Its last layer repeats (middle part 93.8, stretch 167.4), so what scatters here is layers 0 to 2.

## Why the prediction was wrong in size

- **New turns in layers 0 to 2: "I take 0", and 5.5 either way for the range.** This step failed. The turns are worth 12 us ahead of the mark; 6.7 us (early_new) and 10.8 us (early_old) by time. My reason was that the lengths were equal and the end of layer 2 nearly in the same order. Equal counts say nothing of what an order costs, and the end of layer 2, where I looked and saw the same counts, is where the time was won (104 us to 92 between the last send and the mark). Rival 4 had it (1.5% either way, 7% for each), but as a single thing in place of the forecast, not on top of it.
- **The last layer: 15.4 + 6.4 - 1.2 - 1.0 - 3.3 = 16.3.** Measured 182.9 less 167.2 = 15.7. The sum was right, and in part by luck: the masks gave less than their term, the last stretch lost more than its own, and a gain ahead of the 25th exponential that I hadn't summed made up for it. Masks: 13.3 gross and 8.4 to 9.0 net instead of 15.4 and 11.5 (0.06 each holds in many groups; in the third units of the last stretch it is 0.03).
- **One turn of value products, 6.4.** 4 to 6.1, and 0.20 a group in the middle part: right.
- **The end, 1.2.** From the last exponential to the end it is 11.7 us before and 12.1 to 13.3 with the changed last layer: right, as far as the clock, which is partly at half there, lets it be told.
- **Bias, 1.5.** The instructions save 6.2 us, four times what I summed from the chain, and the time 0.4, give or take 3.8.
- **Selects at 0.6 and 0.8, hidden.** They take 0.41 and 0.64, 1.46 us a group instead of 2.0, and TensorE waits 1.3 us in all. Hidden was right. The Trainium skill (GPSIMD Engine Reference, Engine selection) has one-input work at about line rate; my estimate from that, 0.9 a group, is below the 1.46 of the rows. POOL has room for one select a tile and none for two.
- **The last stretch, ScalarE-bound at 1.98.** Wrong mechanism. I had closed the loop over values, exponential and copy. The real one goes over the score banks and the norm: 0.55 + 0.22 + 0.34 + 0.61 + 0.40 + 0.37, 2.49 with the hops 2.54. No gain in this stretch at all; six groups at 2.54 instead of 1.98 cost 3.4 us of the sum. They came back ahead of it. From the mark to the 25th exponential the changed kernel needs 59.3 to 61.3 us where before needs 66.5 to 67.0, and mask_tensor, with the masks, still only 61.6. So most of it isn't the masks, and the new turns, the joined value turns and the six tiles are left for it. Order_only, with 67.3, doesn't fit the turns alone; what it is, is open.
- **15% of the freed time lost, 3.3.** This stood for the question whether the freed time is used, and the answer depends on the order. Under the new one the middle part gives 10.1 of the 12.7 us that masks and value turns are worth there. Under the old one (late_old against early_new) it gives 5.4, and the parts around it take more than that back: stretch 183.1 and 181.2, time 0.9863 and 0.9913, 3.8 us. So over the whole stretch nothing is left, which is more than rival 2 took off. Late_old shows the code without the order, order_only the order without the code, and neither shortens the last layer as a whole.
- **The scale 0.960.** I multiplied the whole sum by it because the profile was 32 us too long. All of that lay ahead of the mark, so the terms of the last layer should have stood as they were: 0.7 us, too little to matter.
- **Rival 3, the queue of fetches.** The chain of late_old shows it; 3 us there at most. In the changed kernel the fetches behind the mark take 30.9 us instead of 25.7 (to 599.8 and to 607.3), but the last one still comes sooner, and mask_tensor, without selects, has 29.8 there: it is the order, not the selects.

What adds up: 12.7 ahead of the mark and 14.5 behind make the 27.2 us between the two profiles. The timed medians differ by 30.5; the changed kernel's profile was its slowest run. Which moves in the order win the 12 us, and why the slower chip gains more, stays open.

## What to carry to other kernels

A hand-written order is part of the change: price the code edits under the order they come with, and mark the work (a fetch, a send) to see where two orders part, because counts of turns don't show it. A change of order and code has to be tried as a pair: the code alone and the order alone each gave nothing in the last layer. Where an instruction is taken out, price it from several groups and not from one; beside a wait it is worth less than where the engine is full. To price a single edit, measure between two counted instructions of a part that runs at full clock and without fetches; it repeated within 0.4 us where whole runs scatter by 6 and more. When TensorE gets free, look for the loop over banks and buffers that was hidden under it, and close each candidate on paper with all its members before believing any engine's sum.

## What the runs showed of the hardware

- The bias product of 10 rows in 32-bit type ahead of full-height ones holds a column block at 1.50 us; with 118 rows of zeros more it takes 1.11.
- POOL's select in place on 32-bit data: 0.41 us for 2 x 128 elements a row, 0.64 for 4 x 128, with single ones up to 1.09.
- Short matmuls of 16-bit type ahead of the 32-bit norm products: four of 128 columns take 0.22 or 0.23 us to the start of the norm in ten groups of the changed kernel, and 0.35 in the last stretch, where the first of them had waited 0.47 us for a bank.
- One change more between full-width products and 32-column strips cost 0.20 us a group in the middle part of values_two.
- TensorE's granted clock fell from 1.00 to half in the last stretch of select_twice, where TensorE had been busy for 5.72 of 8 us and then waited 1.12 us in one piece; in late_old, behind a wait of 6.3 us, it is 0.50 from 590 to 605, in which TensorE is busy for 10.70 of 15 us, half-clock time included:

```profile
590.00:605.00 15.00, 10.70 (x83) 5.13 (x84) 9.46 (x31) 6.53 (x13) 10.52 (x16) 0.50 0.07 20
```

- The changed kernel took 734 us in two sets and 769 us on the chip of the third (before: 764 and 812). All that the changed kernel loses there lies ahead of the mark, with a mean clock of 0.93 against 0.95 and 0.96; the stretch took 166.9 us there and 167.4 and 168.4 in the other two.
